# A decoder layer with 32 experts on one core: the first blocks of four experts are taken from three batch rows and placed in the last row's tail

## What is computed

```python
x = x + attention(layernorm(x))                 # 4 batch rows of 512 tokens, 16 heads of 128
x = x + ssm(context, z=layernorm(x))            # selective scan, 16 states, 512 channels
def ffn(x):                                     # x = layernorm(x), 2048 tokens of 512
    probs = softmax(x @ gate_weight.T)          # 32 experts
    topv, topi = top_k(probs, 8); topv /= sum(topv)
    active = topv * alpha >= 0.05               # with a fallback of one
    w = topv * active; w /= sum(w)
    for e in range(32):
        g, u = split(x @ gate_up[e].T)          # 2 x 192
        out += (silu(g) * u) @ down[e].T * w[:, e]
x = x + ffn(layernorm(x))
```

## Time and profile before

| what | us |
|---|---|
| three runs | 1505.06, 1509.01, 1511.95 (median 1509.01) |
| the profiled execution | 1514.47 |
| its span, first to last instruction | 1512.7 |
| PE busy | 1351.7 (89%) |
| DVE busy | 1106.5 (73%) |
| ACT busy | 936.6 (62%) |
| POOL busy | 477.4 (32%) |

### The profile page before, as it was taken

The page is one execution under the profiler, slowest core; times in us unless marked ns, Lnnn a source line. Parts: engine busy times, 40 slices in busy tenths (PEclk is TensorE's granted clock), DMA queues, the critical chain, the costliest instruction groups (busy, mean ns, idle before and its releaser), DMA issues.

```text
span 1512.7 us, 26288 instructions
## 1 busy us (share of the span) xinstructions
PE 1351.7 (89%) x6762; PEld 994.9 (66%) x6763; DVE 1106.5 (73%) x1581; ACT 936.6 (62%) x2454; POOL 477.4 (32%) x367
## 2 busy tenths in 40 slices
PE   5699899999999999999999999999932889998995
PEld 4377686547888654788765478876431767787775
DVE  4377589849888984988899498878775456776662
ACT  4658785458878545886854588775230456666652
POOL 0000110000022241412224141264404766666664
PEclk9899999999999999999999899999955889999998
DMA  7459997714679761477976147788712479999884
GB/s 243 162 171 259 279 242 174 184 25 130 179 209 227 182 169 37 122 200 197 228 183 158 35 124 196 200 175 207 196 56 55 114 184 238 231 246 230 219 183 54
DMA packets 139563, 260.99 MB, mean 173 GB/s; under 512 B 48717, under 2 KB 50206, under 8 KB 131152
## 3 DMA queue, kind: packets, MB, share of 16 engines
q0 software_dynamic: 36480, 122.30, 37.3%
q1 hardware_dynamic: 76704, 86.70, 19.8%
q10 hardware_dynamic: 26288, 50.87, 10.1%
HBM read 170.57 MB, written 46.21 MB: 143 GB/s over the span
## 4 chain that ended last, share of the span: by engine, by line
PE 53%; DMA 17%; issue 11%; DVE 9%; ACT 6%; POOL 2%; POOLq 1%; ACTq 1%; SPq 1%; DVEq 0%
DMA out<-y_ring,add_ids 12%; PE bank L670 12%; PE bank L693 10%; PE bank L653 6%; PE pair L614 3%; PE pair L616 3%; PE pair L615 3%; PE bank L537 3%; PE pair L537 2%; DMA c_bc<-bc_dram 2%; PE bank L655 2%; DVE dbu L2061 1%; DMA y<-state 1%; PE pair L597 1%; PE bank L657 1%
## 5 line engine op out<-in xcount | busy, mean ns | idle before, releaser
L670 PEld LDWEIGHTS bank<-v_aug,probs 128*128 128x128 f32 x2048 | 237.1, 191 | 22.3 <-ACT probs L1350 16.7
L670 PE MATMUL bank<-v_aug,probs 128*128 128x129 f32 x2048 | 244.2, 275 | 5.1 <-ACT probs L1350 5.1
L2832 POOL DMA_INDIRECT lists<-entry,slot x128 | 198.1, 1547 | 134.4 <-DVE slot L2320 96.7
L693 PE MATMUL bank<-wout,o_t 128*128 128x512 f32 x512 | 231.2, 606 | 4.3 <-issue 4.3
L1359 ACT ACTIVATE decay<-delta,neg_a 128x511 f32<-128x511 f32 x256 | 165.1, 722 | 49.8 <-DVE dbu L2144 31.6
L1350 ACT ACTIVATE probs<-bank 128x512 f32<-128x512 f32 x256 | 153.1, 608 | 63.6 <-PE bank L670 37.7
L693 PEld LDWEIGHTS bank<-wout,o_t 128*128 128x128 f32 x512 | 97.8, 195 | 123.4 <-issue 123.1
L2847 POOL DMA_DIRECT2D y<-dbu x32 | 28.6, 895 | 380.8 <-DVE dbu L2149 272.3
L2144 DVE TENSOR_TENSOR_SCAN dbu<-decay,dbu 128x1024 f32<-128x1024 f32 x64 | 144.6, 2281 | 4.9 <-ACT decay L1359 2.8
L2144 DVE TENSOR_TENSOR_SCAN state<-decay,state 128x1024 f32<-128x1024 f32 x64 | 145.3, 2284 | 2.7 <-ACT decay L1359 0.3
L2941 POOL DMA_INDIRECT out<-y_ring,add_ids x68 | 113.2, 1665 | 90.7 <-DMA out<-y_ring,add_ids 40.7
(11 more groups left out here) (242 smaller groups left out, 2867.8 us busy)
## 6 DMA issues: line engine op xcount, KB each, us to landing
y<-dbu POOLq DMA_DIRECT2D x32, 1024.0 KB
w_raw<-in_w_exp ACTq DMA_DIRECT2D x64, 512.0 KB
wq<-wq_dram POOLq DMA_DIRECT2D x30, 1024.0 KB, 8.7
y<-state POOLq DMA_DIRECT2D x28, 1024.0 KB
wout<-in_wout SPq DMA_DIRECT2D x64, 256.0 KB, 4.8
b_bc<-bc_dram SPq DMA_DIRECT2D x64, 256.0 KB, 3.8
c_bc<-bc_dram SPq DMA_DIRECT2D x64, 256.0 KB, 5.1
lists<-in_const ACTq DMA_DIRECT2D x3, 2904.0 KB, 13.2
```

The lines of the kernel that those rows point to most:

```text
L670: mm = pe.matmul(bank_o[half][:, (t % 2) * (DH + 1):(t % 2 + 1) * (DH + 1)], probs[:, k, t * P:(t + 1) * P], v_aug[:, k, :], start=(k == 0 ...
L693: mm = pe.matmul((bank_o + bank_s)[t][:], o_t[:, h, t * P:(t + 1) * P], wout[:, h % 4, :], start=(h == 0), stop=(h == H - 1))
L2832: pool.indirect_dma_start(out=lists, out_offset=bass.IndirectOffsetOnAxis(ap=slot[:, t, k:k + 1].bitcast(U32), axis=0), in_=entry[:, t, :] ...
```

## The change

- Experts 0 to 3 (`PRE` = 4) each give their first block of 128 tokens from the first three batch rows alone. If an expert had fewer entries there, its count would be raised to 128 (five small matmuls and two DVE steps in the third row's routing).
- SP loads these four lists right behind the last row's output projection (`lists_first`), POOL clears `x_blk` (DVE did), gathers the four blocks (`get_first`) and computes `w_lo` of experts 0 to 3 (`split_low`, DVE did), all ahead of the last row's sends.
- PE, ACT and DVE have the work of blocks 0 to 3 between the steps of the last row's tail and of the count.
- ACT loads expert 3's weights ahead of `gates` and cuts all four experts' weights in the tail, and loads experts 4 to 7 there.
- The remaining blocks of experts 0 to 3 come next (blocks 4 and on), then the other experts. ACT and DVE catch up with the cutting of experts 4 to 6 in `two_experts` and `expert(4, ..., opened=(6,))`.
- POOL's order changes: each of the first adds stands between groups of sends, and the adds of blocks 0 to 7 (`add_next`) always wait for the add before to have landed, as far as it is of the other parity; there is no look in the table.

The core of the diff:

```diff
+PRE = 4
+            def lists_first():
+                sp.wait_ge(S["op_ps"], NB * TT)
+                sp.wait_ge(S["sent"], (NB - 1) * SENT)
+                for r in range(PRE):
+                    load_get(0, r, r * CAP)
+                    load_add(r, r * CAP)
...
@@ load_quad @@
-                    if early and r % MIN_BLK == 0:
+                    if early and q == 1:
+                        sp.wait_ge(S[f"sent{r}"], TT * 16)
+                    elif early and r % MIN_BLK == 0:
                         sp.wait_ge(S[f"sent{(q * QUAD + r) // MIN_BLK}"], TT * 16)
...
@@ ACT, last row @@
                 norm_seed(b, "z")
+                load_expert(3)
                 gates(b)
                 split_expert(2, 0)
+                split_expert(2, 1)
+                split_expert(3, 0)
+                split_expert(3, 1)
                 norm_seed(b, "f")
-                split_expert(2, 1)
+                load_next(4)
+                xt(0)
+                xt(1)
                 out_copy(b, 0)
                 out_copy(b, 2)
                 logit_exps(b)
-                load_expert(3)
+                load_next(5)
+                silu(0)
+                load_next(6)
+                ht(0)
+                silu(1)
...
@@ DVE, last row @@
-                dve.wait_ge(S["oT_ok"], NB * H)
-                split(0, 0)
...
+                xt(0)
                 out_copy(b, 1)
                 out_copy(b, 3)
-                split_rest(0)
-                split(1, 0)
+                xt(1)
                 softmax_top(b)
                 active(b)
+                hidden(0)
                 weights(b)
                 slots(b)
-                split_rest(1)
...
-            dve.memset(x_blk[:], 0.0).then_inc(S["blank_ok"], 1)
+            ht(0)
+            hidden(1)
...
@@ POOL @@
+            def split_low(e):
+                pool.wait_ge(S["whi_ok"], e * 3 + 3)
+                for part in (0, 2, 1):
+                    pool.tensor_tensor(part_w(w_lo, e, part, N_SPLIT), part_w(w_raw, e, part, N_RAW), part_w(w_hi, e, part, N_SPLIT).bitcast(F32),
+                                       ALU.subtract).then_inc(S["wlo_ok"], 1)
...
+            def add_next(blk):
+                q, r = blk // QUAD, blk % QUAD
+                pool.wait_ge(S[f"add_in{r}"], q * 16 + 16)
+                pool.wait_ge(S["yb_ok"], blk + 1)
+                pool.wait_ge(S[f"added{r % 2}"], ADDED0 + blk // 2 * 16)
+                pool.wait_ge(S[f"added{1 - r % 2}"], ADDED0 + (blk + 1) // 2 * 16)
+                add(r)
...
+            pool.wait_ge(S["op_ps"], NB * TT)
+            pool.wait_ge(S["y_ok"], NB)
+            pool.memset(x_blk[:], 0.0).then_inc(S["blank_ok"], 1)
+            pool.wait_ge(S["blank_ok"], 1)
+            pool.wait_ge(S["xf_out"], (NB - 1) * 16)
+            for r in range(QUAD):
+                get_first(r)
+            for e in range(PRE):
+                split_low(e)
             pool.wait_ge(S["slot_ok"], NB)
             pool.wait_ge(S["entry_ok"], NB * 2)
-            send_last(range(0, 3))
+            sends(0)
+            pool.wait_ge(S["x2_out"], NB * 16)
+            add_next(0)
+            sends(1)
             pool.wait_ge(S["xf_out"], NB * 16)
+            get_now(4)
+            sends(2)
...
```

371 lines of the change are left out of this document (247 added, 124 removed).

## The result

The changed kernel takes 1527.02 us (median of 8 runs, 1520.03 to 1540.01) against 1510.49 for the kernel before on the same chip (8 runs, 1505.06 to 1514.75). The ratio is 1.0119, with a 95% interval of [1.0093, 1.0145]: **slower by 18 us**, 14 to 22. The prediction was 1512.6 us, 1500 to 1525: right neither in the size nor in the range. The profiled execution took 1530.27 us, its span is 1528.5; before's was 1514.47 with 1512.7.

A forecast was written before the change was run, and what follows sets the result against it. The expert phase was taken to wait for adds to land about as much as for PE. The terms -1.3 + 1.4 + 0.5 + 3.0 = +3.6 us gave 1518.1 profiled, less 5.5 to the median: 1512.6 us, range 1500 to 1525.

The forecast's parts named there:

- GpSimd's part: In the last row's tail, POOL's 12 subtractions meet DVE's steps: +3 us, between bounds of 0 and 12.2.
- The first send: POOL's first send after the last row's routing: expected at about 1155; past 1160 was a sign of being wrong.
- Rival 1: In the tail, DVE is held for whole POOL instructions: 10 us in place of 3, 1519.6 us; chance 0.25.
- ScalarE's three issues: In the tail, three DMA issues on ACT between the second norm and the gates delay the gates: +1.4 us.
- The chain of POOL and the adds: From the first send, POOL's sends, gathers and adds bring the add of block 10 to 1249.5 from 1250.83: -1.3 us.
- Add of block 6: At the start of the expert phase, issued at 1226.3, some 76 us behind the first send, 6.1 before its old time.
- The add of block 0: On POOL behind the first send: waits 2.6 us for its block's weighing at 1158.5, POOL being ready at 1155.9.
- The gather of block 4: On POOL behind the first send: waits 2.2 us for the table and comes at 1167.7.
- The four landings: Single adds from block 6 to 10 land one after another, 5.8 us each, 5.3 to 6.3 apart.
- Block 14: In the expert phase, weighed within 3 us of 1259.8 plus the first send's shift; behind it nothing is changed.
- Third row's matmuls: In the third row's routing, five small matmuls of at most 0.21 us each at the lower clock: +0.5 us.
- Rivals 2 to 4: Lead kept, 1501.4 us, chance 0.22; GpSimd too slow, 1521, 0.08; gathers or weights late in the tail, 1516, 0.05.

The follow-up runs named there:

- VectorE divides: The changed kernel, but VectorE divides the weights of experts 0 to 3 again and GpSimd none of them: 1514.66 us, ratio 1.0031 to the kernel before.
- early ids: SyncE loads ids for the adds of blocks 4 to 7 before the lists of blocks 8 to 11, in two variants of the changed kernel: 1510.91 and 1511.91 us.
- one at a time: The changed kernel, but GpSimd waits for its own completion after each of the twelve subtractions: 1526.42 us, ratio 1.0124 to the kernel before.
- the kernel before plus six: The kernel before, with six added GpSimd subtractions of the weights of experts 0 and 1 in the tail: 1514.75 us, ratio 1.0042 to the kernel before.
- the changed kernel again: The changed kernel, unaltered, run for a second trace on the slower chip: one run, 1534.04 us.
- pieces of 256: The changed kernel, but GpSimd makes 40 subtractions of 256 columns instead of 12: 1526.30 us on a slower chip, ratio 1.0032 to the kernel before.
- its pair: The kernel "VectorE divides", but blocks 6 and 7 are added in one pair by the table's order: 1512.50 us, ratio 1.0019 to the kernel before.

## Why the prediction was wrong

**GpSimd's part: the step that failed.** The prediction took +3 us "nearer to what the rows show", between bounds of 0 and 12.2. Measured were 16.1 us of holds, above the upper bound, and 13 us of time (1.0119 against 1.0031). Three things were wrong in that term.

- *The bound.* It used VectorE's speed, 1.22 us for 1024 columns. POOL needs 2.3: 23.6 us in all, from 11.66 + 11.90, where 12.2 were put. The estimate from the Trainium skill, 22.5 us (GPSIMD Engine Reference, Performance versus the Vector engine), was 5% off; the sum didn't use it.
- *The weight.* One row in which POOL was the one held was read as "here at POOL's cost". That POOL's DMA issue waits for VectorE told nothing of what VectorE does behind POOL's arithmetic. No row showed either, and the value belonged in the middle at least.
- *The turns.* The prediction thought of holds of one POOL instruction each. In the first run VectorE lost five boundaries in a row, 9.6 us for an instruction of 0.16.

The first send came at 1169.90, past the 1160 that the prediction named as its sign of being wrong; counted from the tail's begin it is 12.4 us later than before, where +4.4 (1.4 + 3.0) was forecast.

**Rival 1 was right** and had 0.25: VectorE is held, for whole instructions. Its size, 10 us, was too small by the same speed. By the sum with the measured holds, 16.1, less the 3.1 that the logits gave back, it would have given 1509.0 − 1.3 + 0.5 + 13.0 = 1521.2: inside the range, and still under the measured 1527. The rule named beside it (Trainium skill, SBUF — State Buffer, Who interferes with whom) says that the two exclude each other for the whole instruction and the later one waits; the second run agrees to 0.01 us (1141.74 and 1141.73), the first run holds for longer than the rule says, six instructions.

**ScalarE's three issues, +1.4.** Right where it shows (+1.3 with VectorE dividing), hidden in the changed kernel behind the longer wait for VectorE.

**The chain of POOL and the adds, −1.3.** The trace has +0.7. Add of block 6: predicted +76.0 behind the first send, +77.3. The add of block 0 didn't wait where 2.6 were put (block 0 was weighed 3.3 behind the first send, 1.9 before its add). The gather of block 4 waited 6.87 us where 2.2 were put, the add of block 4 3.81 for 4.3. The four landings: 23.2 predicted, 23.9. That the lead of four early blocks is gone by block 10 was the prediction's main point on this side, and it holds in every trace without the early ids: 99.6 to 104.6 in all kernels with three-row entries, 97.0 to 100.9 in the three traces with the order of before. Block 14, weighed within 3 us of 1259.8 plus the shift by the forecast, came at 1278.3, where that gives 1279.4; in the second trace, on the slower chip, it stands at +115.3, 6 us later than in the kernel before.

**Third row's matmuls, +0.5.** Not to be seen in scatter of 5 us: 970.16 and 975.13 for the kernel before, 974.99 and 974.74 for the changed one, and 971.72 and 967.34 for "VectorE divides" and "one at a time", which have these matmuls too.

**What stays open.** With VectorE dividing, the ratio is still 1.0031, 0.3 to 9 us, of which the traces show 1.3 in the tail and 0.3 in the chain. And of the 18 us of the changed kernel, 12.0 are the tail's (65.0 in two traces against 52.9); the rest, 2 to 10 us by the interval, has no stretch that shows it.

**Rivals 2 to 4.** The lead wasn't kept (101.25, not under 95). POOL was ready at 1147.7, 21 us before the slots, so GpSimd was not too slow. And blocks 0 to 3 came early as said.

## What to carry to other kernels

An engine that is idle isn't free: GpSimd's arithmetic on SBUF held VectorE's instructions that read two inputs from SBUF, and some with one, and it matters at whose expense it runs, not how long it is idle. If it must share, put its work under VectorE's PSUM reads, statistics and waits: half of the subtractions cost 0.6 to 1.8 us there. Small pieces helped too, but took back only half of the tail's growth. And before work is moved early, look at what the later stretch paces itself by: four blocks done ahead bought nothing that the runs can tell, and the add of block 10 stood some 100 us behind the first send with and without them. Moving that add 6 to 7 us forward didn't move the medians either, so it isn't shown to be the only pace of the end.

## What the runs showed of the hardware that was not expected

- An instruction of 4 columns on VectorE was held 9.79 us (9.16 in a second trace) over five boundaries of GpSimd instructions, in the second run of the same program only to the next one, twice in each trace. GpSimd's own instructions stay at 2.33 to 2.36 us for 1024 columns in the first run, but 2.79 in the kernel before plus six, where VectorE got in between. Which of the two comes first at a boundary the runs don't explain; with a completion wait or pieces of 256 columns no hold was longer than one GpSimd instruction (at most 2.2 and 0.6 us).
- Held were: VectorE's instructions with two inputs in SBUF (L2092, L2094, L2208, L2315, L2320), the step that writes `xf` (L2110, one tensor input, f32), and a cast of 4 columns (L2350). Not held, in the midst of a run: those with an input in PSUM (L2202) and statistics (L2004).
- The logits ran at the upper clock level in the changed kernel (granted 0.93 in the stretch from 1152, 32 matmuls in 3.81 us) and at the lower in the kernel before (0.50 in the stretch from 1130, 6.87 us), though TensorE had stood idle longer in front of the transposes just before them (9.08 us against 5.38). The next matmuls, from 1156.91, ran at 0.50 again. That bought 3.1 us back, here, in the changed kernel again and in "one at a time". The later arrival isn't shown to be the cause: in "pieces of 256" TensorE was idle 5.24 us and the logits took 6.87, and "VectorE divides" and its pair, which are alike up to there, had them at either level (granted 0.50 in the stretch from 1136 and 0.90 in that from 1132):

```profile
1135.80 6.88 PE L787 MATMUL bank<-w_gate,o_t 128*128 128x32 f32 x32
```

```profile
1132.06 4.04 PE L787 MATMUL bank<-w_gate,o_t 128*128 128x32 f32 x32
```

```profile
1152.00:1156.00 4.00, 4.00 (x36) 4.00 (x34) 1.29 (x2) 0.49 (x1) 0.00 (x0) 0.93 0.87 324
1156.90:1161.00 4.10, 4.09 (x12) 3.70 (x12) 3.46 (x24) 1.58 (x2) 0.00 (x0) 0.50 0.67 241
```

(First "VectorE divides", then its pair, then busy time by stretch in the changed kernel, columns as in rows 2: the seventh number is the granted clock.)
